# Router logits of a metaformer block: two 8-column matmuls a slab, or one of 16 columns and a sum on VectorE

## The reference

```python
x = x + conv_ref(_ln_c(x), mask, Wq, Wk, Wv, Wg, Wo, Wb)        # attention
t = to_tokens(x)
def ffn_ref(x, router_w, router_b, expert_w, expert_b):
    router_probs = softmax(x @ router_w + router_b, axis=-1)     # 8 logits a token
    top_p, top_i = top_k(router_probs, 2)
    top_p = top_p / sum(top_p, axis=-1, keepdims=True)
    expert_out = einsum("bnd,edc->bnec", x, expert_w) + expert_b
    gathered = take_along_axis(expert_out, top_i[..., None], axis=2)
    return einsum("bnk,bnkc->bnc", top_p, gathered)
t = t + ffn_ref(_ln_t(t), router_w, router_b, expert_w, expert_b)
```

## Time and profile before

| | |
|---|---|
| runs | 857.56, 859.1, 863.3 us; median 859.1 |
| profiled execution, its own time | 860.74 us |
| its span | 859.0 us |
| TensorE matmuls | 790.4 us busy, 92%, 15372 instructions |
| VectorE | 756.5 us busy, 88%, 1829 instructions |
| GpSimd | 606.2 us busy, 71% |
| ScalarE | 552.0 us busy, 64% |
| L890, the addition of the bias | 40 times, 200 ns each |
| L1231 and L1232, the router's matmuls | 200 each, 166 ns each |

### The profile page before, as it was taken

How to read it: one execution, slowest core, us unless ns; L and a number is a source line. 1 busy time by engine, 2 the same in 40 slices (tenths; PEclk the granted TensorE clock), 3 DMA queues, 4 the chain that set the end, 5 groups by cost and what they waited for, 6 DMA issues and landing times.

```text
span 859.0 us, 39278 instructions
## 1 busy us (share of the span) xinstructions
PE 790.4 (92%) x15372; PEld 533.2 (62%) x15372; DVE 756.5 (88%) x1829; ACT 552.0 (64%) x1369; POOL 606.2 (71%) x990
## 2 busy tenths in 40 slices
PE   1999778899999999999999999999999999999743
PEld 1899345666666666666666666666666666666411
DVE  8998535799999999999999999999999999999664
ACT  3887335577667776777667766777677766776331
POOL 7996001378877787778767887778777876778786
PEclk9999989999999999999999999999999999999965
DMA  4563100000211111111111121111111111111000
GB/s 114 193 206 133 55 16 28 26 26 26 64 34 34 34 57 42 34 34 45 53 34 34 33 64 35 33 34 57 41 34 33 42 57 34 34 37 31 25 9 24
DMA packets 32578, 42.46 MB, mean 49 GB/s; under 512 B 6288, under 2 KB 27280, under 8 KB 32400
## 3 DMA queue, kind: packets, MB, share of 16 engines
q1 hardware_dynamic: 31920, 39.95, 14.4%
q10 hardware_dynamic: 480, 0.02, 0.0%
HBM read 13.74 MB, written 6.55 MB: 24 GB/s over the span
## 4 chain that ended last, share of the span: by engine, by line
PE 78%; POOL 9%; issue 6%; DVE 4%; ACT 2%; DMA 0%; POOLq 0%; DVEq 0%; ACTq 0%
PE psS L1120 11%; PE psS L1095 6%; PE ps_x L1151 6%; PE psS L1127 5%; POOL ln_s L376 3%; PE ps_x L1176 3%; PE ps_r L1176 3%; PE psS L1139 3%; PE ps_x L1179 2%; PE ps_r L1179 2%; PE psS L1100 2%; POOL xn L379 2%; PE ps_m L1084 2%; PE ps_o L1251 2%; PE ps_o L1252 2%
## 5 line engine op out<-in xcount | busy, mean ns | idle before, releaser
L827 DVE TENSOR_REDUCE negm<-psS 128x12 f16<-128x1920 f32 x80 | 146.0, 1825 | 14.0 <-PE psS L1105 9.3
L376 POOL TENSOR_TENSOR ln_s<-ln_s,half 128x5 f32<-128x5 f32 (+1 forms) x60 | 86.1, 1435 | 50.6 <-DVE ln_s L883 44.3
L424 POOL TENSOR_TENSOR add<-prod 128x256 f32<-128x256 f32 x160 | 115.0, 730 | 8.8 <-DVE prod L947 8.7
L429 POOL TENSOR_TENSOR add<-add 128x128 f32<-128x128 f32 x200 | 91.2, 456 | 3.3
L583 ACT ACTIVATE gate<-ps_o 128x320 f32<-128x320 f32 x80 | 35.2, 440 | 88.5 <-PE ps_o L1209 88.4
L540 ACT ACTIVATE pt_b<-psS 128x1920 f32<-128x1920 f32 x40 | 70.9, 1771 | 32.1 <-PE psS L1139 32.1
L395 POOL TENSOR_TENSOR xc<-x,ln_s 128x320 f32<-128x320 f32 x40 | 28.9, 722 | 70.5 <-DVE ln_s L876 70.5
L419 POOL TENSOR_TENSOR og_lo<-og,og_hi 128x320 f16<-128x320 f32 x80 | 63.4, 793 | 18.4 <-ACT og_hi L577 18.4
L431 POOL TENSOR_TENSOR ymix<-add 128x64 f32<-128x64 f32 x200 | 63.9, 320 | 15.7
L619 ACT ACTIVATE kept<-ps_r,coef 128x64 f32<-128x64 f32 x320 | 70.0, 339 | 3.2 <-DVE coef L930 2.4
L1095 PE MATMUL psS<-bm,ident 128*128 128x480 f16 (+1 forms) x320 | 68.6, 338 | 3.2 <-issue 2.0
(11 more groups left out here) (279 smaller groups left out, 2847.1 us busy)
## 6 DMA issues: line engine op xcount, KB each, us to landing
xin<-in_x SPq DMA_DIRECT2D x20, 320.0 KB, 3.0
xs_all<-xs_pair SPq DMA_DIRECT2D x20, 320.0 KB, 2.5
xs_q<-xs_all SPq DMA_DIRECT2D x40, 160.0 KB, 2.1
xs_v<-xs_all SPq DMA_DIRECT2D x40, 160.0 KB, 2.4
xin<-in_x SPq DMA_DIRECT2D x40, 160.0 KB, 2.4
out<-res SPq DMA_DIRECT2D x40, 160.0 KB, 2.1
w_raw<-in_expert_w SPq DMA_DIRECT2D x2, 128.0 KB
eb_raw<-in_expert_b SPq DMA_DIRECT2D x15, 2.0 KB
```

The lines of the kernel that those rows point to most:

```text
L376: pool.tensor_tensor(ln_s[a][:, 3, 0:w], ln_s[a][:, 2, 0:w], half[:, 0:w], ALU.pow).then_inc(own, 1)
L424: pool.tensor_tensor(add1[t % 2][:], prod_of(t)[:, 0:4, :], prod_of(t)[:, 4:8, :], ALU.add).then_inc(mix_step[t], 1)
L429: pool.tensor_tensor(add2[t % 2][:], add1[t % 2][:, 0:2, :], add1[t % 2][:, 2:4, :], ALU.add).then_inc(mix_step[t], 1)
L827: dve.tensor_reduce(negm[c][:, :, 0:slots], psS[:, :, 0:slots * N].rearrange("i h (s j) -> i h s j", s=slots), AX.X, ALU.max, negate=True) ...
```

## The change

The two halves of the weights become the two planes of one tensor, `w_hl`, of 128 x 2 x 1100; `w_hi` and `w_lo` are now names of its planes. The router issues one matmul a slab: its moving operand is the 8 router columns of both planes, 16 columns in two pieces, and its result 16 columns in PSUM, the products with the high half and with the low half side by side. VectorE sums the two over a view of the bank in which they are the innermost dimension (80 elements a partition in, 40 out, into the new tensor `lg_sum`), waits for that on a new semaphore `lg_half`, and adds the bias with both operands in SBUF. lg_done, which frees the bank and starts the routing, is signalled by this addition as before.

```diff
-        w_hi = sb("w_hi", [P, WALL], F16)
-        w_lo = sb("w_lo", [P, WALL], F16)
+        w_hl = sb("w_hl", [P, 2, WALL], F16)
+        w_hi, w_lo = w_hl[:, 0, :], w_hl[:, 1, :]
...
+        lg_sum = sb("lg_sum", [P, T, E])
...
             def logits(g, bank):
 
                 dve.wait_ge(rt_done, g + 1)
-                dve.tensor_tensor(lg[:], bank[:, 0:T * E].rearrange("p (t e) -> p t e", t=T), rb[:], ALU.add).then_inc(lg_done, 1)
+                both = bank[:, 0:2 * T * E].rearrange("p (t s e) -> p t e s", t=T, s=2)
+                dve.tensor_reduce(lg_sum[:], both, AX.X, ALU.add).then_inc(lg_half, 1)
+                dve.wait_ge(lg_half, g + 1)
+                dve.tensor_tensor(lg[:], lg_sum[:], rb[:], ALU.add).then_inc(lg_done, 1)
...
                 take(bank, lg_done, g + 1)
                 pe.wait_ge(xs2_done, g + 1)
                 for t in range(T):
-                    mm(bank[:, E * t:E * t + E], lhsT=xs2[a][:, t, :], rhs=w_hi[:, R0:R0 + E], start=True, stop=False)
-                    end = mm(bank[:, E * t:E * t + E], lhsT=xs2[a][:, t, :], rhs=w_lo[:, R0:R0 + E], start=False, stop=True)
+                    end = mm(bank[:, 2 * E * t:2 * E * (t + 1)], lhsT=xs2[a][:, t, :], rhs=w_hl[:, :, R0:R0 + E], start=True, stop=True)
                 end.then_inc(rt_done, 1)
```

More of the change, by code:

```diff
@@ L181, in build @@
         t2_done, xs2_done = sem("t2_done"), sem("xs2_done")
-        rt_done, lg_done, rt_step, rt_exp, rt_tail = sem("rt_done"), sem("lg_done"), sem("rt_step"), sem("rt_exp"), sem("rt_tail")
+        rt_done, lg_half, lg_done, rt_step, rt_exp, rt_tail = sem("rt_done"), sem("lg_half"), sem("lg_done"), sem("rt_step"), sem("rt_exp"), sem("rt_tail")
         ct_done, ct_evac, cb_done, base_done, res_done = sem("ct_done"), sem("ct_evac"), sem("cb_done"), sem("base_done"), sem("res_done")
```

## The result

The changed kernel took 866.56 us in the median (863.41 to 867.51), beside 859.1 for the kernel before (857.56 to 863.3). The ratio is 1.0068, 95% interval 1.0047 to 1.0089: slower by 0.7%, or 5.8 us (4.0 to 7.6). The ratio is made from all the times of both kernels; the two medians alone lie 7.5 us apart. The forecast was 864.7, slower by 5.6 us on the same level.

What follows compares the result with a forecast made beforehand. TensorE and VectorE were both almost always busy, the router's addition nearly on TensorE's path. A loss of 0.15 us a step made 36 x 0.15 + 0.2 = 5.6 us, from 859.1 to 864.7 us; range 859.5 to 871.

Steps and rivals of the forecast that it cites:

- The removed matmuls: Router on TensorE: five matmuls and five loads a step fewer, 0.025 us per 16-column matmul, 0.12 us saved a step.
- Rival 4: Router: 16-column matmul in two pieces costs double, TensorE saves nothing, 0.27 us a step, 869 us; 0.21 shared with rival 2.
- Of the 0.12 us, 0.03 is left there.: Projection into ps_x waits for ScalarE's v_main, can't start before 457.54, so TensorE keeps only 0.03 us.
- The reduction, the wait: VectorE's logits: reduction of 80 elements into 40 takes 0.25 us; the addition starts 0.04 us behind its end.
- The addition: VectorE's bias addition with both operands in SBUF beside GpSimd: 0.26 us, low end 0.20, high 0.36.
- Rival 2: Reduction and addition: slower beyond 1%, the addition meets GpSimd; 0.33 us a step, 871.2 us; 0.21 shared with rival 4.
- TensorE's path: Projection into ps_r waits for lg_done: matmul at 457.99 against 457.84, 0.15 us later a step.
- rival 1: Wait and addition are cheap, bank ps_r ready just in time: 0.00 to 0.05 us a step, 860.4 us; chance 0.17.
- rival 3: Faster: lg_done doesn't hold the load, gain of 0.03 to 0.12 us a step kept, 856.5 us; chance 0.06.
- VectorE's path: Weigh to next step's first maximum: 0.23 us later, 0.11 covered, 0.12 comes through.
- the larger of the two counts, not their sum: Step loss is the larger of TensorE's 0.15 us and VectorE's 0.12 us: 0.15.
- The end: After 800 us, the four routers left can lose some 0.2 us each, at least the last does; 0.2 in all.

Runs made afterwards that it cites:

- experiment 2: Changed kernel with one VectorE addition of bias to the high columns from PSUM, low products left out: 855.04 us against 858.66 before, ratio 0.9943.
- experiment 5: Changed kernel with two additions, each with one operand in PSUM, instead of reduction and SBUF addition: ratio 1.0022 to the kernel before, step 17.50 us.
- experiment 6: Changed kernel with the bank freed by the reduction and the bias addition moved behind the weigh: ratio 1.0054 to the kernel before, step 17.59 us.
- Experiment 4: Changed kernel with bank ps_r freed by the reduction (lg_half) instead of the addition: ratio 1.0056 to the kernel before, step 17.59 us.
- experiment 12: Changed kernel with bias put into the bank by a TensorE matmul, VectorE's reduction alone, one setup instruction fewer: 856.1 us against 859.45 before, ratio 0.9969.
- experiments 10: Changed kernel with bias put into the bank by a TensorE matmul, VectorE's reduction alone, 20 small VectorE instructions added in the setup: ratio 1.0027 to before.
- experiments 11: Changed kernel with bias put into the bank by a TensorE matmul, VectorE's reduction alone, 40 small VectorE instructions added in the setup: ratio 1.0032 to before.
- kernels 1: Kernel before with only the weights' halves as planes of one tensor and lg_sum allocated, unused: 860.11 us against 858.66, ratio 1.0012.
- 3: Changed kernel with ten matmuls of 8 columns again, the halves side by side in the bank, VectorE as changed: ratio 1.0085 to the kernel before.

## Why the prediction was right

The time and the direction were right, 5.6 us forecast and 5.8 measured. By its steps:

- **The removed matmuls.** Taken: 0.025 us for a matmul of 16 columns, 0.12 saved. Measured: five starts in 0.13 us, the step 0.11 shorter in experiment 2. Rival 4 (double cost) is out.
- **"Of the 0.12 us, 0.03 is left there."** This step failed. I had taken ScalarE's handoff from the router's load (0.12 + 0.03 us). For v_main it is 0.05 + 0.00, in the changed kernel (456.57 to 456.62) as in experiment 2, and the whole 0.11 us is kept when nothing is added. "A gain on TensorE alone is small" was false: it is 0.57% of the kernel. The error didn't reach the sum, because the sum starts from the router's results and not from this bound.
- **The reduction, the wait.** 0.25 taken, 0.24 measured (231 to 242 ns). The addition starts at 456.81, 0.04 behind the reduction's end, as taken, while the weigh, which waits for nothing of its own engine, starts 0.08 before the end of the addition. The Trainium skill ("VectorE: DVE Perf Modes", section "The DRAIN you can't avoid") would have the wait cost nothing; these rows speak against it a second time.
- **The addition.** 0.26 taken, median 0.27 measured. The reason (GpSimd beside two operands in SBUF) is borne out by experiments 5 and 6. Rival 2 had the right mechanism and the wrong place: the long delays fall on the comparison behind it (0.72 us in most steps) and on the addition only where it is moved (0.56). The forecast had no term for the comparison.
- **TensorE's path.** Forecast: the projection at 457.99 - 457.05 = 0.94 us behind the router. Measured 0.91, since the handoff took 0.05 and not 0.08. Lateness 0.12 a step instead of 0.15. With that rival 1 (the bank ready just in time) and rival 3 are out. As a sign of this wait the forecast named 0.1 to 0.2 us in nearly every step; the waits view has 0.38 (5.7 us in 15), since it counts the load's idle time and not the delay of the matmul.
- **VectorE's path, "0.12 comes through", and "the larger of the two counts, not their sum".** The forecast let VectorE's lateness of 0.23 us through to the maximum unchanged and covered 0.11 of it. It wasn't unchanged: 0.24 at the weigh, 0.69 behind the comparison, 0.27 at the maximum, of which some 0.13 was covered. In experiment 5 a lateness of 0.11 at the weigh is 0.02 at the maximum. That 0.23 was near to the 0.27 at the end is luck. Experiment 4 has VectorE's path alone: 0.11. Both together make 0.14. A sum would have been 0.23. So the larger counts, with 0.02 or 0.03 from the other.
- **The end.** 0.2 taken for the last four routers. From the last steady addition to the end it is 861.6 - 791.36 = 70.2 us after and 69.6 before, so 0.7, by one execution of each.
- **Total.** 36 x 0.14 + 0.7 = 5.7 us, where the forecast had 36 x 0.15 + 0.2. That the two sums agree within 0.1 us is luck as well: TensorE's path was taken 0.03 a step too high, the part of VectorE's path that comes on top (0.02) was left out, and the end was taken 0.5 too low.

So the forecast's mechanism held in its main step: TensorE's gain is spent before the bank comes free, by two VectorE instructions in series. What it didn't see is that the gain would have been kept whole had VectorE stayed at one addition (experiment 2, whose logits lack the low products), and that most of VectorE's lateness hangs on what GpSimd does beside the comparison behind the logits: 0.69 us behind it in the changed kernel, 0.05 in experiment 5.

## What to carry to other kernels

When TensorE's work is made cheaper by handing a sum to VectorE, price the dependent pair and not the instruction: here 0.24 + 0.04 + 0.27 us against one addition of 0.20, with 0.11 us to pay it from. A constant that VectorE adds behind a matmul can be put into the accumulation by one more matmul: here that cost TensorE 0.03 us, and the step of experiment 12 is 17.38 us against 17.47 before. Its matmul stood behind the wait for the tokens; whether it costs nothing ahead of that wait wasn't tried. Where two SBUF operands can't be avoided, look in the timeline at what GpSimd has under way at that moment, for the added instruction and for those that it shifts. And don't take a handoff from one pair of engines at one place for the same pair elsewhere.

## What the runs showed of the hardware that I had not expected

- A VectorE instruction of 40 elements with both operands in SBUF took from 0.19 to 0.60 us in one kernel, and ended 0.05 to 0.06 us behind the GpSimd instruction beside it in most steps; with one operand in PSUM it took 0.20 us forty times. In the steady stretch of the changed kernel none of 374 VectorE instructions with two SBUF operands that started beside a GpSimd instruction ended before it.
- VectorE stalled by about 0.35 us once in 128 of its instructions (records of the trace, semaphore instructions included). The place follows the count of the instructions from the start of the program (experiments 10 to 12), and it costs 0.20 to 0.26 us a time where a short instruction stands ahead of it and nothing in the step behind a long one. A kernel with VectorE near its limit can move by 0.4% when one instruction is added to its setup. That also limits what the ratios in the table say of 0.1 or 0.2%: before and kernels 1 and 2 have 2,858 VectorE instructions in the trace and so the same position, while the changed kernel and 3 to 6 have one more a step (2,898), so that the position wanders; no idle time but that before og stands in the changed kernel's steady steps.
- The handoff from ScalarE's end to a waiting load was 0.05 us at one place and 0.11 to 0.12 at another, 0.4 us apart in the same step.
